# Head attention with v packed by query quarters, sums of six tiles added on GpSimd, one tile of values in a single step, and maxima split after their turn

## The reference, cut to what matters

```python
x = _L0_conv_ref(x, ...)                        # attention over 1024 pixels, 4 images, 256 channels
t = _to_tokens(x)
t = t + _L1_attn_ref(_ln_t(t), ...)             # the stage of the change
t = t + _L1_ffn_ref(_ln_t(t), ...)              # 8 experts, one per token

def _L1_attn_ref(x, ...):                       # B, N, C = 4, 1024, 256; H = 8 heads, d = 32
    ...
    scores = jnp.einsum('bnhd,bmhd->bhnm', q, k) * (1.0 / np.sqrt(d))
    attn = jax.nn.softmax(scores, axis=-1)
    vals = jnp.einsum('bhnm,bmhd->bnhd', attn, v).reshape(B, N, C)
    return vals @ w_proj + b_proj + x
```

## Time and profile before

| | |
|---|---|
| time, median of 3 runs | 1323.62 us (1322.67 to 1324.68) |
| the profiled execution | 1324.85 us, its span 1323.0 us |
| PE matmul busy | 1219.5 us, 92% of the span |
| PE weight load busy | 772.7 us, 58% |
| DVE busy | 682.5 us, 52% |
| ACT busy | 420.2 us, 32% |
| POOL busy | 207.6 us, 16% |
| mean granted TensorE clock | 0.950 of full speed |

### The profile page before, as it was taken

One profiled execution on the slowest core, in us unless ns is written; L12 is line 12 of the kernel. 1 busy time (PEld: TensorE's weight loads), 2 busy tenths in 40 slices (PEclk: granted clock), 3 DMA queues, 4 the chain that ended last, 5 costly groups with the idle time before them and its releaser, 6 DMA issues. The chain is left out here.

```text
span 1323.0 us, 21162 instructions
## 1 busy us (share of the span) xinstructions
PE 1219.5 (92%) x6723; PEld 772.7 (58%) x6724; DVE 682.5 (52%) x1540; ACT 420.2 (32%) x465; POOL 207.6 (16%) x418
## 2 busy tenths in 40 slices
PE   6899999895999999999999999998971999999995
PEld 3677676663534444444443444434861899999995
DVE  3265455446666666666666666652862333333331
ACT  1312132220255555555555555553210111111110
POOL 0002030302000000000000000000054244434442
PEclk8899999795999999999999999998965999999998
DMA  6203353131532332323323322205636565656551
GB/s 196 56 2 118 132 171 128 64 127 64 201 102 53 90 83 76 96 64 96 93 63 90 83 55 64 64 9 158 216 140 159 169 207 188 210 185 211 194 199 64
DMA packets 97141, 156.78 MB, mean 119 GB/s; under 512 B 44848, under 2 KB 65264, under 8 KB 96464
## 3 DMA queue, kind: packets, MB, share of 16 engines
q1 hardware_dynamic: 86576, 121.81, 30.1%
q0 software_dynamic: 9712, 31.35, 7.4%
q10 hardware_dynamic: 816, 3.15, 0.7%
HBM read 108.77 MB, written 44.06 MB: 116 GB/s over the span
## 5 line engine op out<-in xcount | busy, mean ns | idle before, releaser
L215 DVE TENSOR_REDUCE s_nmax<-h_ps_m 128x1 f32<-128x512 f32 x488 | 314.4, 686 | 178.2 <-PE h_ps_m L209 177.7
L928 ACT ACTIVATE h_expd<-h_ps_e 128x1024 f32<-128x1024 f32 x256 | 261.9, 1024 | 237.4 <-PE h_ps_e L946 232.6
L962 PE MATMUL h_ps_o<-h_expd,h_ones 128*32 128x512 f32 x1024 | 270.7, 604 | 0.0
L962 PE MATMUL h_ps_o<-h_expd,s_vh 128*32 128x512 f32 x1024 | 270.7, 604 | 0.0
L1559 PEld LDWEIGHTS ps_h<-xs_c,lnt 128*128 128x128 f32 x1248 | 148.2, 195 | 4.8 <-issue 2.9
L1559 PE MATMUL ps_h<-xs_c,lnt 128*128 128x128 f32 x1248 | 148.6, 278 | 2.3 <-DVE xs_c L1511 2.3
L1569 PE MATMUL ps_y<-w,vals_t 128*128 x624 | 141.2, 379 | 0.6 <-DVE ys L1524 0.6
L578 PE MATMUL a_ps_v<-a_val,a_expd 128*128 128x257 f32 x512 | 120.0, 388 | 5.1 <-ACT a_expd L456 4.5
L1569 PEld LDWEIGHTS ps_y<-w,vals_t 128*128 128x128 f32 x624 | 115.5, 190 | 15.1 <-issue 1.0
L1600 ACT ACTIVATE vals_t<-ps_h 128x1024 f32<-128x1024 f32 x39 | 39.9, 1024 | 263.3 <-DVE ps_h L1504 263.3
L1504 DVE TENSOR_TENSOR ps_h<-ps_h,b_t 128x1024 f32<-128x1024 f32 x39 | 48.1, 1233 | 131.5 <-PE ps_h L1559 131.5
(11 more groups left out here) (188 smaller groups left out, 1421.9 us busy)
## 6 DMA issues: line engine op xcount, KB each, us to landing
lnt<-in_w SPq DMA_DIRECT2D x39, 1024.0 KB, 4.8
qk_scr<-a_head_hi SPq DMA_DIRECT2D x16, 512.0 KB, 2.7
qk_scr<-a_head_lo SPq DMA_DIRECT2D x16, 512.0 KB, 3.6
w<-in_w POOLq DMA_DIRECT2D x8, 1024.0 KB, 6.1
xs<-xs_scr SPq DMA_DIRECT2D x39, 128.5 KB, 2.0
a_x_t<-in_x_t POOLq DMA_DIRECT2D x4, 1024.0 KB, 10.4
r_scr<-a_res POOLq DMA_DIRECT2D x4, 1024.0 KB, 6.0
v_scr<-res SPq DMA_DIRECT2D x4, 1024.0 KB, 3.9
```

Source lines behind the costliest of these rows:

```text
L215: self.nc.vector.tensor_reduce(self.nmax[k][:, nb, half:half + 1], ps_m[:, half, :], AX.X, ALU.max, negate=True).then_inc(self.v_max, 1)
L928: nc.scalar.activation(expd[:, m % RING, :], flat(ps_e[m % 2]), ACT.Exp, scale=SCALE).then_inc(a_exp, 1)
L962: mm = nc.tensor.matmul(ps_o[k][c:c + D, :], w, expd[:, m % RING, half * HALF:(half + 1) * HALF], start=(m == 0), stop=(m == NB - 1))
```

## The change

- `values` packs `ps_o` otherwise: the four strips are the four quarters of the queries, columns 0 to 255 hold v, columns 256 to 511 the sums. A matmul has 256 columns in place of 512.
- GpSimd adds the exponentials of tiles 0 to 5 (`ADDED` = 6) with five additions of 128 x 1024 into `added`. PE multiplies by ones only tile 6, tile 7 and `added`.
- `expd` has 8 buffers in place of a ring of 4; ACT also waits for GpSimd before it writes one of the first six again.
- Steps 0 and 1 of a head have values and sums of tiles 6 and 7 of the head before, step 2 the sums of its `added`, step 3 values of tiles 0 and 1, steps 4 to 7 values of one tile. `outputs` moves from step 3 to step 5, and before the values there; the norm on DVE likewise.
- The maxima run 14 blocks ahead: steps 0 and 1 serve the next head, steps 2 to 7 the one after. Their minimum (`least`) is one reduce in place of three instructions; the turn on PE moves to the end of step 1; ACT writes hi after its second exponential, DVE subtracts to get lo after step 2's reduces.
- In `conv_phase`, `HEAD_BLOCKS` is 2, 2, 2, 2, 2, 1, 1, 1, 1.
- SP writes the maxima rows first, then loads, and has the `w2` loads too, one each four heads, from a `w2` whose rows are laid out by partition on the host.

```diff
-LEAD = NB + NB // 2
+LEAD = 2 * NB - 2
+QUARTER = N // 4
+ADDED = 6
@@ Heads
+    def least(self, dve, t, j, first=False):
...
+        self.nc.vector.tensor_reduce(self.nmaxes[:, :], nm[:, :, :], AX.X, ALU.min).then_inc(self.v_mh, 1)
     def max_turn(self, pe, dst, ident, t, j):
-        pe.wait_ge(self.v_split, SLOTS * t + j + 1)
-        self.nc.tensor.transpose(dst[0:2 * NB, 0:P], raw(self.msplit[:, :]), ident[:, :]).then_inc(self.pe_maxt, 1)
+        pe.wait_ge(self.v_mh, SLOTS * t + j + 1)
+        self.nc.tensor.transpose(dst[0:NB, 0:P], self.nmaxes[:, :], ident[:, :]).then_inc(self.pe_maxt, 1)
+    def row_hi(self, act, src, t, j, first=False):
...
+        self.nc.scalar.activation(self.mrow[0][:, :], src[0:NB, 0:P], ACT.Copy).then_inc(self.a_mrow, 1)
+    def row_lo(self, dve, src, t, j):
+        dve.wait_ge(self.a_mrow, SLOTS * t + j + 1)
+        self.nc.vector.tensor_tensor(self.mrow[1][:, :], src[0:NB, 0:P], raw(self.mrow[0][:, :]), ALU.subtract).then_inc(self.v_mrow, 1)
@@ conv_phase
-        HEAD_BLOCKS = (2, 2, 2, 1, 1, 1, 1, 1, 1)
+        HEAD_BLOCKS = (2, 2, 2, 2, 2, 1, 1, 1, 1)
@@ head_phase, gpsimd
+                def head(t, j, first=False, left=SLOTS):
+                    h, total = SLOTS * t + j, added[j % 2]
+                    for m in range(1, ADDED):
+                        pool.wait_ge(a_exp, NB * h + m + 1)
...
+                            pool.wait_ge(g_add, (ADDED - 1) * h + m - 1)
+                        nc.gpsimd.tensor_tensor(total[:, :], (expd[:, 0, :] if m == 1 else total[:, :]), expd[:, m, :],
+                                                ALU.add).then_inc(g_add, 1)
@@ head_phase, tensor
+                def values(j, m):
+                    for q in range(4):
+                        mm = nc.tensor.matmul(ps_o[j % 2][q * D:(q + 1) * D, 0:QUARTER], vh[j % SLOTS][:, m, :],
+                                              expd[:, m, q * QUARTER:(q + 1) * QUARTER], start=(m == 0), stop=(m == NB - 1))
...
+                def sums(j, e, done, last=False):
+                    for q in range(4):
+                        mm = nc.tensor.matmul(ps_o[j % 2][q * D:(q + 1) * D, QUARTER:2 * QUARTER], ones[:, :],
+                                              e[:, q * QUARTER:(q + 1) * QUARTER], start=False, stop=last, skip_group_check=True)
...
+                    for i in range(NB):
+                        step_scores(i)
+                        step_maxima(i)
+                        if i < 2:
+                            if not first:
+                                tail(j - 1, ADDED + i)
+                            if i == 1:
...
+                                    hd.max_turn(pe, ps_o[j % 2], ident, t, j + 1)
+                        else:
+                            if i == 2 and not first:
+                                all_sums(t, j - 1)
+                            if i == 5 and not first:
+                                outputs(t, j - 1)
+                            if i == 3:
...
+                                    pe.wait_ge(hd.v_mrow, h + 2)
+                                values(j, 0)
+                            if i >= 3:
+                                values(j, i - 2)
```

More of the change, by code:

```diff
@@ L811, in _ @@
                         if g == NB - 1:
-                            hd.split_max(dve, 0, 0, first=True)
+                            hd.least(dve, 0, 0, first=True)
+                    if (part, n) == (heads_qk, 2):
+                        hd.row_lo(dve, ps_v[:, 0, :], 0, 0)
 def head_phase(nc, io, keep, sems, hd):
@@ L826, in head_phase @@
         stk, vh = hd.stk, hd.vh
-        expd = sb("expd", [P, RING, N])
+        expd = sb("expd", [P, NB, N])
+        added = [sb(f"added{k}", [P, N]) for k in range(2)]
         osum = sb("osum", [P, HALF])
@@ L955, in outputs, with tail, all_sums, step_scores @@
                     last.then_inc(pe_ot, 1)
[L957 to L964, removed]
+                def values(j, m):
+                    for q in range(4):
+                        mm = nc.tensor.matmul(ps_o[j % 2][q * D:(q + 1) * D, 0:QUARTER], vh[j % SLOTS][:, m, :],
+                                              expd[:, m, q * QUARTER:(q + 1) * QUARTER], start=(m == 0), stop=(m == NB - 1))
+                    if m < ADDED:
+                        mm.then_inc(pe_pv, 1)
+                def sums(j, e, done, last=False):
+                    for q in range(4):
+                        mm = nc.tensor.matmul(ps_o[j % 2][q * D:(q + 1) * D, QUARTER:2 * QUARTER], ones[:, :],
+                                              e[:, q * QUARTER:(q + 1) * QUARTER], start=False, stop=last, skip_group_check=True)
+                    mm.then_inc(done, 1)
+                def tail(j, m):
+                    values(j, m)
+                    sums(j, expd[:, m, :], pe_pv)
+                def all_sums(t, j):
+                    pe.wait_ge(g_add, (ADDED - 1) * (SLOTS * t + j + 1))
+                    sums(j, added[j % 2], pe_sum, last=True)
                 def head(t, j, first=False, left=SLOTS):
                     h = SLOTS * t + j
-                    for i in range(NB):
+                    def step_scores(i):
                         if i == 0:
@@ L980, in head @@
                                 pe.wait_ge(*hd.loaded(stack_in, 16 * STACK_DMAS, t, j + 2))
[L981 to L987, removed]
@@ L996, in _ @@
                 stream(pe, head)
-                for m in range(NB - LAG, NB):
-                    pe.wait_ge(a_exp, NB * (HEADS - 1) + m + 1)
-                    values(SLOTS - 1, 1, m)
+                pe.wait_ge(a_exp, NB * HEADS)
+                for m in range(ADDED, NB):
+                    tail(SLOTS - 1, m)
+                all_sums(HEADS // SLOTS - 1, SLOTS - 1)
                 outputs(HEADS // SLOTS - 1, SLOTS - 1)
@@ L1021, in head @@
                     for i in range(NB):
-                        ahead = 1 if i < NB // 2 else 2
+                        ahead = 1 if i < 2 else 2
                         if left >= ahead:
[L1024 to L1029, removed]
+                            hd.block_max(dve, ps_m, NB * h + LEAD + i, (j + ahead) % 2, (i + LEAD) % NB)
+                        if i == 1 and left >= 1:
+                            hd.least(dve, t, j + 1)
+                        if i == 2 and left >= 1:
+                            hd.row_lo(dve, ps_o[j % 2], t, j + 1)
+                        if i == 5 and not first:
+                            norm(t, j - 1)
                 stream(dve, head)
```

95 lines of the change are left out of this document (48 added, 47 removed).

## The result

The changed kernel takes 1291.07 us, median of 4 runs (1288.57 to 1292.35); the kernel before took 1324.15 us on the same chip (1322.67 to 1325.22, 4 runs). The ratio is 0.9749, 95% interval 0.9729 to 0.9768. The profiled execution took 1292.35 us, its span is 1290.4 us.

What follows compares the result with a forecast made beforehand. PE was taken to bound the head stage. From the profiled 1324.85 us, heads 1 to 29 give -42.6, conv tail +7.4, head 0 +1.1, the end -2.3: 1288.4, taken as 1288 us, range 1273 to 1309.

Steps and rivals of the forecast that it cites:

- The plain step: Head stage, a step with one set of values: PE time forecast at 1.70 us, against 2.12 before.
- Rival (3): PE in the heads: issuing the shorter matmuls binds, 18.1 us per head, 1357 us; chance 0.04.
- the reduced form of it, about 1308: PE in the heads: issue limits in part, 0.25 us per 256-column pass, kernel still faster, near 1308 us; chance 0.07.
- Rival (5): PE values and sums: four strips with different inputs no longer run side by side, over 1410 us; chance 0.02.
- the wait of step 1: Each head, before the turn of maxima: PE waits for DVE's small reduce, 0.55 us forecast, bounds 0.3 and 0.8.
- the forecast's -1.47: Head stage: each head takes 15.9 us, 1.47 less than before; -42.6 us over heads 1 to 29.
- that term: End of the head stage, head 30 to the last turn: GpSimd's adds set the pace, 29.4 us, -2.3 us.
- rival (4): GpSimd in the heads: adds slowed by exponentials written beside them bind from 3.4 us each, about 1500 us at doubled time; chance 0.02.
- the single costs: One-time effects outside heads 1 to 29: conv tail +7.4, head 0 +1.1, end -2.3 us.
- The wait in the conv tail: Conv parts 3 and 4, last image: heads_qk held behind the second block's reduces, 3.7 us per part, +7.4 us.
- rival (1): Conv tail: idle PE makes the clock fall once or twice, 3.5 us per fall, 1292 to 1295 us; chance 0.23.
- two of the forecast's signs: Expected in the trace: heads_qk of conv parts 3 and 4 start 7.5 us apart, head 0's first scores near 363.

Runs made afterwards that it cites:

- the two variants: Two kernels on the changed one with the later turn and the blocks at the end: GpSimd adding seven tiles, 1254.91 us, or all eight, 1331.91 us.
- the filler: Changed kernel plus three matmuls of 128x512, result unread, on PE before the second block of conv parts 3 and 4: 1289.05 us.

## Why the prediction was right

**Passes go by columns.** The pass of 256 columns was taken at 0.22 between 0.215 and 0.32. The plain step came out at 1.69 for 1.70, and two passes removed gave 0.23 each. The sets at the end of head 31 of the kernel after start at 871.02, 871.48, 871.91 and 872.34, 0.43 for two passes: 8 pairs of weight load and matmul, one each 0.054 us. Rival (3) and the reduced form of it, about 1308, are excluded by that: no limit on issue shows down to this spacing. The Trainium skill (TensorE: Matmul & The Clock Gate, section "Wait — 56ns, not 53.3ns?") gives about 62 ns per matmul with hardware decode off. No such limit is seen in this kernel: its trace has matmul records at 54 ns, 16 of them from 871.48 to 872.34. Whether hardware decode was on, no run here shows. Rival (5) goes with it: four strips with four different inputs run side by side as before.

**The packing is not the gain.** With the sums back on PE the kernel is slower than before. All of the gain is the five sets of sums per head, 10 passes of 256 columns, that left PE for an engine that had nothing to do. They are 2.15 us at 0.215, and 17.38 - 15.33 = 2.05 as measured with the turn out of the way; the wait of step 1 takes 0.53 of them back, and the remaining 1.5 per head is the forecast's -1.47.

**The new wait was where and as long as worked out.** 0.55 forecast, 15.86 - 15.33 = 0.53 measured by moving the turn.

**POOL fits, by its measured duration.** Half of a 128 x 2048 addition plus a gap gave 2.35; it is 2.44 (9.77 us for four). In the middle that is free. At the end it is not: the first of the last ten additions starts 4.0 us after head 30's first scores, as forecast, and the ten take 25.0 and not 24, so the last sums start at 29.0 for 28.2, and that term was 1 us too good. That rival (4) was rightly placed is shown by the two variants: 14.6 us of additions fit in 14.87, 17.0 set the pace. The threshold is PE's head divided by the number of additions: an estimate of 14.87 / 6 = 2.48 us for six of them, against 2.44 measured.

**What was too small: the single costs.** Their sum was forecast at +6.2 and is +13.2. The wait in the conv tail was right, 7.2 for 7.4. What was missing is the clock, which the forecast had as rival (1) at 3.5 us per fall and 0.23: it fell twice and cost 4.5 us in all, 2.0 and 2.5. It should have been in the sum, as the likelier case: a stretch of idle time with hardly a matmul in it had been seen to bring the clock down, here were two, and each of the four traces with these waits has at least one fall. For the same reason two of the forecast's signs did not come: the next heads_qk start 9.6 us apart and not 7.5 (7.66 with the filler), and head 0's first scores stand at 367.4 and not near 363. Head 0 was the second miss: its wait for slot 2 lasted to 374.73 - 367.42 = 7.3 us for 7.0 (the line names no releaser; at the same place the version with seven tiles has PE released by the load of vh), but the clock was at one half from about 368.6 until about 379, which the forecast did not consider at all. That is most of the 1.7 us of difference. Why it falls there is open: it falls in head 0 of every variant traced, and in the changed kernel before the wait for slot 2 begins, while the kernel before has the same 2.3 us of idle time ahead of head 0 and keeps its clock. The heads' own gain, 1.8 larger than forecast, and 1.3 us behind the last turn, which is within what that part varies by (411.4 to 415.9 us over these traces), hide nearly half of the miss: that the forecast was only 3 us off is in part luck.

## What to carry to other kernels

When one engine is full and another empty, count in the full engine's own currency (here passes by columns) what can go over, and set against it the other engine's measured duration times count: the change pays as long as that sum stays under the new, shorter period, and it turns into a loss within one more instruction (six additions 1255 us, seven 1332). Whatever crosses engines should be asked for a step later than it is made: moving one small transpose by one step was worth half the gain of the whole change again. Work that is moved to a lead-in stage must stand where the in-order queues have nothing behind it: two small blocks cost 12 us in the traced execution, clock included, in the middle of a chain of projections, and a third of that at either end of it.

## What the runs showed of the hardware

GpSimd's addition of 128 x 1024 in float32 takes 2.37 to 2.38 us, 2.44 from one to the next where each waits for the last, and keeps this beside PE, ACT and DVE at 98, 56 and 70% of their time; DVE's reduces of 128 x 512 out of PSUM stay at 686 ns beside it. Around the two idle stretches of 2.66 us in the conv tail, with 6 to 7 us of dense matmuls ahead of each, the granted clock of the changed kernel fell to 1.2 GHz from 2.4 (about 338 to 341 and 345 to 351.5 us); with the filler in them it stayed at 2.4. It is not the same in every execution: the two heads_qk behind them took 5.29 and 6.10 us in the changed kernel, 3.60 and 5.29 with the later turn and with seven tiles, 5.29 and 3.60 without additions.
